# Step two of a graph attention layer: the spread's third group ahead of the first turn on TensorE, ScalarE's adjacency check ahead of its first copy of a turned group

## What is computed

```python
h = relu(layernorm(x))
S = adj + eye;  Rf = S / S.sum(1)[:, None];  Rb = S / S.sum(0)[:, None]
Xf = Xb = Xa = h
for s in range(2):                                  # step one, step two
    logits = (Xa @ W1) @ W2 @ (Xa @ W3).T
    A = softmax of the logits kept by a top-p rule (p = 0.9), row by row
    Xf, Xb, Xa = Rf @ Xf, Rb @ Xb, A @ Xa
    Z += Xf @ U1[s] + Xb @ U2[s] + Xa @ U3[s]
x = x + layernorm(h + Z) * gamma + beta
```

## Time and profile before

| | before |
|---|---|
| median of 3 runs | 2401.57 us |
| the profiled execution | 2400.98 us |
| its span, first to last instruction | 2399.2 us |
| mean granted TensorE clock | 0.948 of full speed |
| TensorE busy | 2164.6 us (90%) |
| VectorE busy | 2058.9 us (86%) |
| ScalarE busy | 1946.5 us (81%) |

### The profile page before, as it was taken

How to read it: one execution, slowest core, us unless ns; L and a number is a source line. 1 busy time by engine, 2 the same in 40 slices (tenths; PEclk the granted TensorE clock), 3 DMA queues, 4 the chain that set the end, 5 groups by cost and what they waited for, 6 DMA issues and landing times.

```text
span 2399.2 us, 25921 instructions
## 1 busy us (share of the span) xinstructions
PE 2164.6 (90%) x8250; PEld 1420.6 (59%) x8250; DVE 2058.9 (86%) x3856; ACT 1946.5 (81%) x2824; POOL 748.5 (31%) x935
## 2 busy tenths in 40 slices
PE   7599999999999998799759999999999999999985
PEld 4367767777777777444335555555555555555564
DVE  5699999999999998344399999999999999999975
ACT  5899999999999995233689898998998989989944
POOL 2132443334333341000033333323333333233333
PEclk9799999999999999899879999999999999999997
DMA  5334543445434441321101212212112122221142
GB/s 196 86 98 103 123 121 93 107 111 123 107 98 107 119 109 38 105 62 46 57 24 50 42 50 52 52 52 43 50 50 42 50 52 50 54 42 50 52 119 69
DMA packets 77981, 183.19 MB, mean 76 GB/s; under 512 B 11665, under 2 KB 57872, under 8 KB 77840
## 3 DMA queue, kind: packets, MB, share of 16 engines
q1 hardware_dynamic: 56800, 125.48, 16.3%
q0 software_dynamic: 18720, 54.53, 13.4%
q10 hardware_dynamic: 2320, 1.48, 0.2%
HBM read 154.19 MB, written 27.28 MB: 76 GB/s over the span
## 4 chain that ended last, share of the span: by engine, by line
DVE 30%; PE 12%; ACT 5%; POOL 4%; issue 1%; DVEq 0%; POOLq 0%; ACTq 0%
DVE s_junk L1514 12%; PE bank L871 5%; PE bank L897 4%; DVE s_small L1558 3%; DVE s_logits L1550 3%; DVE s_logits L1678 3%; DVE s_small L1456 3%; POOL s_small L1367 3%; ACT s_junk L1153 3%; PE bank L887 1%; PE bank L859 1%; DVE s_small L1539 1%; DVE s_small L1542 1%; PE bank L933 1%; DVE s_small L1561 1%
## 5 line engine op out<-in xcount | busy, mean ns | idle before, releaser
L1514 DVE SCALAR_TENSOR_TENSOR s_junk<-s_logits,s_small,s_expd 128x3327 uint8<-128x3327 f32 x208 | 766.4, 3685 | 5.5
L897 PE MATMUL bank<-h_aug,s_attT 128*128 128x256 f32 x2704 | 635.6, 384 | 0.9 <-ACT s_attT L1175 0.9
L871 PE MATMUL bank<-both,s_adj 128*128 128x512 f32 x1352 | 609.8, 596 | 28.8 <-ACT s_sides_out L1196 28.7
L897 PEld LDWEIGHTS bank<-h_aug,s_attT 128*128 128x128 f32 x2704 | 513.3, 193 | 114.6 <-issue 47.8
L871 PEld LDWEIGHTS bank<-both,s_adj 128*128 128x128 f32 x1352 | 251.5, 190 | 304.7 <-issue 260.5
L871 PE MATMUL bank<-h_aug,s_adj 128*128 128x257 f32 x1352 | 351.2, 411 | 27.2 <-ACT s_spread_out L1182 27.2
L871 PEld LDWEIGHTS bank<-h_aug,s_adj 128*128 128x128 f32 x1352 | 268.9, 205 | 115.8 <-ACT s_spread_out L1182 45.7
L1112 ACT ACTIVATE s_junk<-s_expd,s_small 128x3327 int8<-128x3327 f32 x104 | 319.8, 3075 | 2.8 <-POOL s_small L1346 1.8
L1106 ACT ACTIVATE s_junk<-s_expd,s_small 128x3327 int8<-128x3327 f32 x104 | 319.2, 3069 | 1.8
L859 PE MATMUL bank<-KTr,QT 64*128 64x512 f32 (+1 forms) x728 | 234.4, 627 | 57.7 <-DVE s_logits L1448 47.3
L1175 ACT ACTIVATE s_attT<-bank 128x512 f32<-128x512 f32 (+1 forms) x364 | 192.1, 562 | 101.5 <-PE bank L887 87.3
(11 more groups left out here) (233 smaller groups left out, 2658.3 us busy)
## 6 DMA issues: line engine op xcount, KB each, us to landing
s_adj<-adj_turned SPq DMA_DIRECT2D x104, 832.0 KB, 5.3
s_adj_total<-adj_turned POOLq DMA_DIRECT2D x52, 832.0 KB, 8.2
z<-s_sides_out POOLq DMA_DIRECT2D x52, 128.0 KB, 3.4
spread<-s_spread_out SPq DMA_DIRECT2D x26, 128.5 KB, 2.9
m_spread_in<-spread SPq DMA_DIRECT2D x26, 128.5 KB, 2.2
attended<-s_att_out SPq DMA_DIRECT2D x26, 128.0 KB, 5.5
m_att_in<-attended SPq DMA_DIRECT2D x26, 128.0 KB, 2.2
z<-m_z_out SPq DMA_DIRECT2D x26, 128.0 KB, 1.7
```

The lines of the kernel that those rows point to most:

```text
L871: done = pe.matmul(SX[:, 0:width], half(t, h)[:, bass.ts(jj, P)], rows_of(j), start=(j == 0), stop=(j == T - 1))
L897: last = pe.matmul(AB[:, 0:D], attT[i % 4][:, b, :], h_aug[:, g + b, 0:D], start=(g + b == 0), stop=(g + b == T - 1))
L1514: chain.did(dve.scalar_tensor_tensor(junk[:, 0:N], logits[t % 3][:, 0:N], col(t, "cand"), expd[t % NE][:, 0:N], ALU.is_gt, ALU.mult, accum ...
```

## The change

In step two's loop alone, two queues get another order. No instruction is added, none is taken away, and no semaphore wait is changed. On TensorE spread 2 goes ahead of turn 0, spread 3 stands behind turn 2 and ahead of multiply 0, and spread 4 takes the place in which spread 3 was. The new order is: logits 0 and 1; spread 0, 1; logits 2 to 6; **spread 2**; turn 0, 1, 2; **spread 3**; multiply 0; turn 3; multiply 1; **spread 4**; multiply 2; turn 4, 5; multiply 3; spread 5; turn 6; multiply 4; spread 6; multiply 5, 6. On ScalarE the two checks go ahead of the copy of turned group 0, and the copy of group 1 goes behind the exponentials, together with that of group 2.

```diff
@@ TensorE, step two
+                            if present:
+                                spread(t, 2)
                             if previous:
                                 turn(t - 1, 0)
                                 turn(t - 1, 1)
                                 turn(t - 1, 2)
+                            if present:
+                                spread(t, 3)
+                            if previous:
                                 multiply(t - 1, 0)
                                 turn(t - 1, 3)
-                            if present:
-                                spread(t, 2)
-                            if previous:
                                 multiply(t - 1, 1)
                             if present:
-                                spread(t, 3)
+                                spread(t, 4)
                             if previous:
                                 multiply(t - 1, 2)
                                 turn(t - 1, 4)
                                 turn(t - 1, 5)
-                            if present:
-                                spread(t, 4)
-                            if previous:
                                 multiply(t - 1, 3)
@@ ScalarE, step two
-                            turned(0)
                             if present:
                                 check(t, 0)
                                 check(t, 1)
-                            turned(1)
+                            turned(0)
                             if following:
                                 exponentials(t + 1)
-                            turned(2)
+                            turned(1, 2)
```

## The result

The kernel after takes **2395.12 us** (median of 9, 2393.24 to 2397.24). The kernel before, timed beside it, takes 2403.21 us (median of 9, 2399.70 to 2404.99). The ratio is 0.997 with a 95% interval of 0.9961 to 0.998, so the change gains 0.2 to 0.4%.

A forecast was written before the change was run, and what follows sets the result against it. VectorE was taken to bound the loop at 43.39 us per plain iteration; only the extra 5.1 us would go, all else 0: 2401.57 - 5.1 = 2396.5 us. Forecast range 2394.8 to 2397.7; 8 in 10, 2394.6 to 2402.5.

The forecast's parts named there:

- The bound: Step two's loop: VectorE sets the plain iteration at 43.39 us; TensorE has 40.9 us of work and 2.5 to spare.
- the 5.1 us: Step two's 24 iterations: time beyond 43.39 us each, put into five iterations, expected to go with TensorE's late logits.
- plain iteration: Step two's loop: an iteration of 43.39 us from one keep of VectorE to the next, expected to stay unchanged.
- TensorE's new timeline: TensorE in the loop: spread 2 covers the 2.50 us wait, leaving two or three short ones of 0.5 to 1.3 us.
- K: Start of VectorE's keep in an iteration; K+4.8 means 4.8 us after that start.
- ScalarE's lead: ScalarE in the loop: exponentials 1.6 us earlier, probes and read_sides 1.0 earlier or not at all; VectorE gains nothing.
- Rival 3: ScalarE doesn't lead: GpSimd's prepared holds the probes, no change, 2400 to 2402 us; chance 0.23 together with rival 1.
- Two ways to the same sum: TensorE's clock in the loop: stays full, or falls costing up to 2.9 us within 3.7 of slack; both remove 5.1.
- Rival 1: Clock falls move to the short wait ahead of spread 0, part stays: 2398 to 2401 us; chance 0.23 with rival 3.
- rival 2: Short waits ahead of spread 0 and among logits drop the clock, TensorE becomes the bound: 2402 to 2411 us; chance 0.14.
- The first tile's start and step one are untouched: Kernel's part ahead of step two's plain loop: claimed unchanged by the reorder, 0 us.
- the tail: Kernel's end: TensorE's last products end some 3 us sooner; bounds -1.4 to +1.0 us, taken as 0.

The follow-up runs named there:

- the filled wait: Five matmuls with discarded results put into TensorE's wait ahead of turn 0, iterations 2 to 25, against the kernel before: 2398.67 us, ratio 0.9981.
- two versions on VectorE: Against after: VectorE's small steps interleaved, 2403.62 us (1.0000 to before); the same with GpSimd's count_needed steps moved to VectorE, 2394.31 us (0.9976 to before).
- The second set: One of three sets of timed runs; the unchanged kernel before had a median of 2403.71 us (27 runs) in it.

## Why the prediction was right, and where only its sum was

**The bound, and the 5.1 us.** VectorE bounds the plain iteration; it stayed at 43.39 in after and with 1.3 us of load on TensorE, and moved only with 3.9. The extra iterations came from the falls of the clock, as the filled wait shows. Of the 5.1 us the change removed 4.7: I had counted the 43.74 iteration's 0.35 among them, which the clock has nothing to do with. The extra stands in six iterations and not in five: what I took for one of them is this one and the next, of 44.21.

**TensorE's new timeline.** Put: turn 0 at K+4.8, 1.2 us of waiting ahead of spread 0, gaps among the logits, 0 to 0.6 at multiply 1 and 0 to 1.5 at multiplies 3 to 5. Measured: K+4.26, 1.05, 0.42, and nothing at the multiplies (0.3 us in the whole loop). The logits end at K+0.7, inside the bounds. The work of 40.9 us is confirmed, as 40.8.

**ScalarE's lead.** Put: exponentials at K+7.4, `read_sides` 1.0 earlier, nothing for VectorE. Measured: K+7.43, 1.3 earlier, nothing for VectorE. Rival 3 is out. What the prediction lacked is that the two halves carry each other: it priced both as free, and alone they cost 3 and 92 us. The terms that I had to hand, 0.61 us of room on ScalarE and the copy that multiply 0 needs, would have given both signs.

**Two ways to the same sum.** I left open whether the clock stays full or falls into slack. It stays full: no slow turns in after's loop. Rival 1 (moved falls, 2398 to 2401) and rival 2 did not happen in this kernel: with 1.05 and 0.42 us of waiting per iteration, in all of them, the clock never fell. But neither is ruled out for other kernels. In the two versions on VectorE the same order of TensorE meets waits of up to 1.27 us among its logits, and there the clock falls in 9 and in 6 of 24 iterations, once behind 1.00 us, shorter than the 1.24 of the earlier trace rows. So the place and the mechanism of rival 2 do occur, and its price does not: those falls cost VectorE almost nothing, as rival 1 had it (0 to 0.4 us each). The rule named beside rival 2 (the Trainium skill, page "TensorE: Matmul & The Clock Gate", section "A second HAM failure mode: psum-queue depth-cycling"), on groups of matmuls with brief idle times between them, describes what these two traces show and not what after's does. (The 2402 at which rival 2's range starts is four of 24 iterations by its own price, one in six and not one in four.)

**The two ends.** Here the sum failed. "The first tile's start and step one are untouched" was put at 0 and is +2.3 us in the profiles; the tail was taken at 0 with bounds of -1.4 to +1.0 and is -3.0. The two misses cancel to -0.7, so that the profiled total of -5.4 lies close to the -5.1 of the sum: that closeness is luck. The start is no effect of the change: the last keep of step one, before anything that was changed, comes at 920.05 us in before and at 922.67 in after, 2.6 later, and from there to the first keep of step two it is 314.98 and 314.66. In all the profiles that last keep of step one lies between 920.05 and 925.18. The tail is the term that was mis-sized. Its bounds looked at the last turns alone; the clock of the later L916 and L933 groups, which made 1.56 us, was in no row that I had read.

**The size.** The medians differ by 8.1 us, the profiles by 5.4. Counted from the last keep of step one to the end, the two profiles of before take 1479.2 and 1478.5 us and those of after 1471.1 and 1472.2: 6.2 to 8.1 less, of which the loop is 4.7 and the end 3.0. The second set agrees: the near copies of after stand 6.0 and 6.2 us below before (three more matmuls; old orders in iteration 25), and after itself, once, 6.6. So 5.1 was too little by the end's 3.0, and the point of 2396.5 came within 1.4 us of the measured median in part because its base, 2401.57, was 1.6 below the 2403.21 that before had beside after.

## What to carry to other kernels

Fill an engine's longest single wait with work that is ready, even where the engine is not the bound: what the wait costs is in what follows it, at half the clock, and that can cross the slack. Then read the granted clock again after every later change, on other engines too: shorter waits elsewhere brought falls back in the two versions on VectorE, and only the room behind them hid it. When two queues are reordered together, price each reorder alone first: if either one loses, note what in the other one it leans on, because that is where the pair will break. And before steps are pulled forward on VectorE, look at which small steps of GpSimd then fall under a full pass.

## What the runs showed of the hardware that I had not expected

- **Falls of the clock can repeat.** Of 26 starts of turn 0 in before 13 are slow, and a second execution has them in the same iterations, though neighbouring iterations have the same 2.50 us wait. In step one the low stretches of the two lie elsewhere. Longer stillness doesn't cost more: behind 8.82 us the slow groups took less (2.82 + 2.64) than behind 3.73 (2.82 + 3.52).
- **The length of a wait doesn't tell whether a fall follows.** Waits of 2.50, of 1.27 and of 1.16 us stand in these traces with a fall behind them and without one.
- **Products nobody needs can pay.** Five matmuls per iteration in the wait, 2.4 us of work, took 3.7 us off the whole (interval 2.4 to 6.7, by the ratio).
- **A small GpSimd step beside VectorE's full pass is held for the length of the pass:** 3.70 us for 0.26. The Trainium skill, page "SBUF — State Buffer", section "Who interferes with whom", says that these two engines share a pair of ports which one instruction holds whole; the trace agrees, with the 3.70 us against a pass of 3.69. It is no rarity here. In each plain iteration of after settle's first step (L1365) starts within a pass and ends with it, 3.31 us on the way to `keep`, and the fifth of `prepare`'s six steps (L1342) takes a mean of 3.46. The first step of `prepare` was held in before (mean 2.52 us), and the earlier exponentials brought it out from under the pass (0.50): that is most of the 59.8 us of GpSimd above.
